# Moving the experts' ranks and marks, and the layer norm's small steps, from VectorE to GpSimd

## The reference

```python
x = x + 0.5 * _L0_ffn_ref(_layernorm(x), ...)      # F
x = x + _L0_attn_ref(_layernorm(x), ...)           # R
x = x + 0.5 * _L0_ffn_ref(_layernorm(x), ...)      # F
x = x + 0.5 * _L1_ffn_ref(_layernorm(x), ...)      # E
x = x + _L1_attn_ref(_layernorm(x), ...)           # M
x = x + 0.5 * _L1_ffn_ref(_layernorm(x), ...)      # E
```

```python
logits = jnp.einsum('bsd,ed->bse', x, router_w) + router_b
probs = jax.nn.softmax(logits, axis=-1)
weights = jnp.max(probs, axis=-1)
top1 = jnp.argmax(probs, axis=-1)
y_all = jnp.einsum('bsd,eod->bseo', x, expert_w) + expert_b
y = jnp.take_along_axis(y_all, top1[:, :, None, None], axis=2)[:, :, 0, :]
out = y * weights[:, :, None]
```

## Time and the profile before

| | us |
|---|---|
| median of 3 runs | 1591.86 (1585.59 to 1592.55) |
| profiled execution, own time | 1587.52 |
| its span, first to last instruction | 1585.8 |
| granted TensorE clock, mean | 0.993 |

### The profile page before, as it was taken

How to read it: one execution, slowest core, us unless ns; L and a number is a source line. 1 busy time by engine, 2 the same in 40 slices (tenths; PEclk the granted TensorE clock), 3 DMA queues, 4 the chain that set the end, 5 groups by cost and what they waited for, 6 DMA issues and landing times. The chain is left out here.

```text
span 1585.8 us, 43554 instructions
## 1 busy us (share of the span) xinstructions
PE 1527.1 (96%) x15760; PEld 910.0 (57%) x15760; DVE 1264.2 (80%) x2662; ACT 934.4 (59%) x1826; POOL 934.7 (59%) x806
## 2 busy tenths in 40 slices
PE   7999999999999899799999999999998899999998
PEld 4666666666666666566666666666663334444443
DVE  7976777777877788786776777768779889999968
ACT  6755555555655433365555555556553378888843
POOL 2865756657664299875756657657446334444454
PEclk9999999999999999999999999999999899999999
DMA  4300000000001243200000000000001212111112
GB/s 163 104 11 5 7 0 7 7 0 7 5 5 34 46 83 76 42 5 5 8 1 7 7 0 7 3 4 8 2 15 28 47 36 61 36 42 46 26 35 67
DMA packets 74636, 43.40 MB, mean 27 GB/s; under 512 B 54106, under 2 KB 71162, under 8 KB 74372
## 3 DMA queue, kind: packets, MB, share of 16 engines
q1 hardware_dynamic: 74500, 41.60, 10.9%
HBM read 10.47 MB, written 2.10 MB: 8 GB/s over the span
## 5 line engine op out<-in xcount | busy, mean ns | idle before, releaser
L642 POOL TENSOR_TENSOR scratch<-scratch 128x512 f16<-128x512 f32 x379 | 440.9, 1164 | 375.4 <-ACT scratch L850 375.0
L845 ACT ACTIVATE scratch<-psum 128x512 f32<-128x512 f32 x512 | 305.2, 597 | 398.0 <-PE psum L2008 397.1
L1420 DVE SCALAR_TENSOR_TENSOR scratch<-psum,scratch 128x512 f32<-128x512 f32 x512 | 352.4, 689 | 234.8 <-PE psum L2008 212.4
L2050 PE MATMUL psum<-ffn_down_hi,scratch 128*128 128x128 f16 x2048 | 369.3, 219 | 0.3
L2051 PE MATMUL psum<-ffn_down_lo,scratch 128*128 128x128 f16 x2048 | 369.4, 219 | 0.0
L2052 PE MATMUL psum<-ffn_down_hi,scratch 128*128 128x128 f16 x2048 | 369.4, 219 | 0.0
L850 ACT ACTIVATE scratch<-scratch 128x512 f16<-128x512 f32 x512 | 318.6, 622 | 9.0 <-DVE scratch L1420 8.9
L2050 PEld LDWEIGHTS psum<-ffn_down_hi,scratch 128*128 128x128 f16 x2048 | 200.3, 98 | 58.9 <-DVE scratch L1427 0.5
L2051 PEld LDWEIGHTS psum<-ffn_down_lo,scratch 128*128 128x128 f16 x2048 | 200.4, 98 | 58.1
L2052 PEld LDWEIGHTS psum<-ffn_down_hi,scratch 128*128 128x128 f16 x2048 | 200.4, 98 | 0.0
L2006 PE MATMUL psum<-x_hi,ffn_gate_hi 128*128 (+1 forms) x512 | 194.5, 380 | 1.5 <-ACT scratch L845 1.5
(11 more groups left out here) (230 smaller groups left out, 2663.7 us busy)
## 6 DMA issues: line engine op xcount, KB each, us to landing
scratch<-scratch SPq DMA_DIRECT2D x96, 128.0 KB, 2.7
raw<-in_ffn_w_dram SPq DMA_DIRECT2D x8, 768.0 KB, 4.3
ffn_up_hi<-scratch SPq DMA_DIRECT2D x32, 128.0 KB, 2.8
x_tok<-in_x_dram SPq DMA_DIRECT2D x8, 256.0 KB, 6.8
out_dram<-x_tok SPq DMA_DIRECT2D x7, 256.0 KB, 2.3
raw<-in_lin_dram SPq DMA_DIRECT2D x1, 1092.0 KB
x_hi<-scratch SPq DMA_TRANSPOSE x46, 2.3
x_lo<-scratch SPq DMA_TRANSPOSE x46, 2.3
```

Source lines behind the costliest of these rows:

```text
L642: pool.tensor_tensor(h_lo[r], h32[r], h_hi[r], ALU.subtract).then_inc(s_plo, 1)
L845: act.activation(gate_act[k % 2], bank(k % 2), ACT.Silu, scale=W_DOWN).then_inc(s_s, 1)
L1420: dve.scalar_tensor_tensor(h32[k % HSLOTS], bank(5 + k % 2), W_DOWN, gate_act[k % 2], ALU.mult, ALU.mult).then_inc(s_h, 1)
L2050: pe.matmul(dst, h_hi[r][:, cols], hi, start=k % FC == 0 and n == 0, stop=False, skip_group_check=True)
```

## The change

1. For the batches from 2 on of either E phase, GpSimd makes e_rank (in two instructions: is_ge, then times rev_index) and e_not (`mark_others`, now a subtraction, first minus rank). VectorE keeps the maximum e_first in the same place (`first_of`). For batches 0 and 1 VectorE still does all three. E_OUT falls from 2^14 to 2^12, since the difference replaces a 0 or 1.
2. ln_neg is gone: the norm on GpSimd subtracts the mean as it stands in ln_mv. This holds in R, E and M.
3. In E and M, ln_var is made by GpSimd just ahead of ln_rstd (`prep_rstd(n, True)`).
4. In GpSimd's iteration, `rank`, `x_lower`, `not_chosen` and then `add` follow one another; before it was `add`, `x_lower`.

```diff
-            def prep_rstd(n):
+            def prep_rstd(n, var=False):
+                if var:
+                    pool.wait_ge(s_mv, n + SUB)
+                    pool.tensor_scalar(ln_var[:], ln_mv[:, 1:2 * SUB:2], LN_EPS, None, ALU.add).then_inc(s_var, SUB)
                 pool.wait_ge(s_var, n + SUB)
...
+                def rank(b):
+                    pool.wait_ge(s_esh, b + 1)
+                    pool.wait_ge(s_efirst, b)
+                    pool.tensor_scalar(e_rank, e_shift, 0.0, None, ALU.is_ge).then_inc(s_etop, 1)
+                    pool.wait_ge(s_etop, b // NB * (NB - 2) + b % NB - 1)
+                    pool.tensor_tensor(e_rank, e_rank, con_("rev_index"), ALU.mult).then_inc(s_erank, 1)
+
+                def not_chosen(b):
+                    pool.wait_ge(s_efirst, b + 1)
+                    pool.wait_ge(s_eoutp, b)
+                    mark_others(pool).then_inc(s_enot, 1)
...
                 for b in range(NB):
+                    if b and b + 1 < NB:
+                        rank(use * NB + b + 1)
+                    if b and b + 2 < last:
+                        x_lower(n0 + SUB * (b + 2))
+                    if b and b + 1 < NB:
+                        not_chosen(use * NB + b + 1)
                     if b:
                         add(b - 1)
-                        if b + 2 < last:
-                            x_lower(n0 + SUB * (b + 2))
                     if b + 3 < last:
-                        prep_rstd(n0 + SUB * (b + 3))
+                        prep_rstd(n0 + SUB * (b + 3), True)
                         norm(b + 3)
...
-                if negate:
-                    dve.tensor_scalar(ln_neg[:], ln_mv[:, 0:2 * SUB:2], -1.0, None, ALU.mult)
-                dve.tensor_scalar(ln_var[:], ln_mv[:, 1:2 * SUB:2], LN_EPS, None, ALU.add).then_inc(s_var, SUB)
+                if var:
+                    dve.wait_ge(s_mv, n + SUB)
+                    dve.tensor_scalar(ln_var[:], ln_mv[:, 1:2 * SUB:2], LN_EPS, None, ALU.add).then_inc(s_var, SUB)
...
+                def first_of(b):
+
+                    dve.wait_ge(s_erank, b + 1)
+                    dve.wait_ge(s_enot, b)
+                    dve.tensor_reduce(e_first, by(e_rank, SUB), AX_X, ALU.max).then_inc(s_efirst, 1)
...
-                        if k == 1 and more:
-                            select(b0 + b + 1)
+                        if k == 1 and more and b == 0:
+                            select(b0 + 1)
+                        if k == 1 and more and b:
+                            first_of(b0 + b + 1)
```

More of the change, by code:

```diff
@@ L332, in build, with mark_others @@
         s_erows_in, s_erows, s_ebias = sem("e_rows_loaded"), sem("e_rows_set"), sem("e_bias_rows_placed")
+        s_etop, s_erank, s_efirst = sem("e_at_top"), sem("e_ranked"), sem("e_first_found")
         s_estep = sem("e_routing_step")
-        E_STEPS = 4
+        E_STEPS = 2
+        def mark_others(engine):
+            rank = e_rank.rearrange("p (q o e) -> p q o e", q=SUB, o=1).to_broadcast([P, SUB, P // E_GROUP, E])
+            first = e_first.rearrange("p (q o c) -> p q o c", q=SUB, o=1).to_broadcast([P, SUB, P // E_GROUP, E])
+            return engine.tensor_tensor(e_not.rearrange("p (q o c) -> p q o c", q=SUB, c=E_GROUP)[:, :, :, 0:E], first, rank, ALU.subtract)
         def expert_banks(t):
@@ L692, in norm @@
                     for q in range(SUB):
-                        ins = pool.tensor_scalar(x_norm[:, q * P:(q + 1) * P], sub(x_tok, SUB * (bx % NB) + q), ln_neg[:, q:q + 1],
-                                                 ln_rstd[:, q:q + 1], ALU.add, ALU.mult)
+                        ins = pool.tensor_scalar(x_norm[:, q * P:(q + 1) * P], sub(x_tok, SUB * (bx % NB) + q), ln_mv[:, 2 * q:2 * q + 1],
+                                                 ln_rstd[:, q:q + 1], ALU.subtract, ALU.mult)
                     ins.then_inc(s_xn, SUB)
@@ L1322, in _, with prep_bn @@
         def _(dve):
-            def prep_bn(n, s):
+            def prep_bn(n, s, after=False):
+                if after:
+                    dve.wait_ge(s_mv, n)
                 for q in range(SUB):
@@ L1628, in route @@
                     dve.tensor_tensor(by(e_shift, SUB), by(bank(7, 0, SUB * E), SUB), over(e_max, SUB, E), ALU.subtract).then_inc(s_esh, 1)
+                def first_of(b):
+                    dve.wait_ge(s_erank, b + 1)
+                    dve.wait_ge(s_enot, b)
+                    dve.tensor_reduce(e_first, by(e_rank, SUB), AX_X, ALU.max).then_inc(s_efirst, 1)
                 def select(b):
                     dve.wait_ge(s_esh, b + 1)
[L1633 to L1636, removed]
+                    dve.scalar_tensor_tensor(e_rank, e_shift, 0.0, con_("rev_index"), ALU.is_ge, ALU.mult).then_inc(s_erank, 1)
+                    first_of(b)
+                    dve.wait_ge(s_efirst, b + 1)
                     dve.wait_ge(s_eoutp, b)
-                    rank = e_rank.rearrange("p (q o e) -> p q o e", q=SUB, o=1).to_broadcast([P, SUB, P // E_GROUP, E])
-                    first = e_first.rearrange("p (q o c) -> p q o c", q=SUB, o=1).to_broadcast([P, SUB, P // E_GROUP, E])
-                    dve.tensor_tensor(e_not.rearrange("p (q o c) -> p q o c", q=SUB, c=E_GROUP)[:, :, :, 0:E], rank, first, ALU.not_equal).then_inc(s_enot, 1)
+                    mark_others(dve).then_inc(s_enot, 1)
                 def invert_sum(b):
@@ L1644, in invert_sum @@
                     dve.tensor_reduce(e_sum, by(e_exp, SUB), AX_X, ALU.add).then_inc(s_estep, 1)
-                    step(b, 4)
+                    step(b, 2)
                     dve.wait_ge(s_eprob, b)
```

24 lines of the change are left out of this document (11 added, 13 removed).

## The result

The changed kernel takes 1605.21 us (median of 6 runs, 1603.88 to 1607.45); the kernel before on the same chip takes 1592.12 (6 runs, 1585.59 to 1592.55). The ratio is 1.009, 95% interval 1.0072 to 1.0107: 0.9% slower, where 0.46% faster was forecast. The profiled execution took 1605.68 with a span of 1603.9, 18.1 longer than the span before; the medians differ by 13.1, since the profiled execution of the kernel before was 4.6 faster than its median.

A forecast was written before the change was run, and what follows sets the result against it. The prediction took VectorE to bound the steady E iteration; savings of 4.31 us in the first E phase and 3.04 in the second, 7.35 together, took 1591.86 to 1584.5 us (-0.46%), range 1578.0 to 1589.5.

The forecast's parts named there:

- What GpSimd adds: Step pricing GpSimd's E iteration after the change: 5.2 plus 0.95 and two waits of 0.10, 6.35 us, under 6.98.
- the forecast loop: Steady E iteration after the change, closed over TensorE and VectorE: 6.98 us, with VectorE waiting about 0.5 before the first pick.
- VectorE is the bound of the steady iteration: Step on the kernel before: VectorE has no idle time in the 7.63 us E iteration, TensorE some 0.8 us of room.
- first E phase to batch 7's first pick: Forecast saving of 4.31 us: 3.13 from five loops of 6.98 and 1.18 in the last iteration.
- second E phase, second pick of iteration 1 to the last first pick: Forecast saving of 3.04 us, with iteration 1 losing 0.14 and loops without statistics taking 6.65.
- the moved add delays nobody: In GpSimd's E iteration, the add behind the marks costs nothing, since its batch's store and reuse are a batch away.
- The prediction's other estimate: GpSimd prices by the skill's 2.6 cycles per element at 1.2 GHz: e_not 0.28 us, the product 0.07.
- the slack ahead of `others`: Time by which GpSimd's marks precede TensorE's `others` in E: 0.20 us, some 0.3 by the skill's cycle rule.
- rival (a): GpSimd's small instructions have a fixed part of some 0.3 us, `others` waits 0.40 per loop: 1588.6 us; chance 0.22.
- the limit of 0.98: In the E iteration, GpSimd's three small pieces together must stay within 0.98 us or `others` waits; forecast 0.80.
- (b): Rival: GpSimd's small pieces cost over 0.54 us each, making it slower; at 0.8 each, 1600 us; chance 0.06.
- (d): Rival: VectorE and GpSimd block each other in E, so the move gives nothing: loop 7.6, 1591 us; chance 0.05.

The follow-up runs named there:

- b: Kernel before with part 2 of the change alone (GpSimd's norm subtracts the mean from ln_mv, ln_neg gone): 1604.86 us, ratio 1.0086.
- c: Kernel before with only the operation of GpSimd's norm changed, add to subtract, operand still ln_neg: 1602.69 us, single run.
- d: Kernel before with only the operand of GpSimd's norm changed, from ln_neg to the mean in ln_mv, still an add: 1587.32 us, single run.
- e: Changed kernel with GpSimd's norm adding the mean from ln_mv instead of subtracting it: 1582.79 us, ratio 0.9964.
- j: Changed kernel with multiply and add in GpSimd's norm in place of subtract and multiply: 1580.04 us, single run.
- k: Changed kernel with multiply and then subtract in GpSimd's norm in place of subtract and multiply: 1608.4 us, single run.
- l: Kernel before with a quarter of GpSimd's norm left out (three of four pieces): 1580.03 us, single run.
- i: Kernel before with ln_var and ln_neg moved to GpSimd, ranks and marks still on VectorE, norm adding ln_neg: 1592.05 us, ratio 1.0025.
- h: Kernel before with ranks and marks moved to GpSimd, ln_neg and ln_var still on VectorE, norm adding ln_neg: 1584.0 us, ratio 0.9981.
- g: f with the add of iteration 6 of the first E phase put behind the power and the norm: 1583.3 us, ratio 0.9973.
- f: Changed kernel with GpSimd itself making ln_neg and the norm adding it, computing the reference's outputs: 1582.49 us, ratio 0.9962.
- m: g with batch 2 of the second E phase ranked and marked by VectorE instead of GpSimd: 1582.97 us, ratio 0.9973.

## Why the prediction was wrong

**The step that failed.** The part "What GpSimd adds" put GpSimd's iteration together "from starts (1.12 + 1.70 + 1.22 + about 1.12)" plus 0.95. The 1.70 is the norm in its old form. Part 2 of the change gives it another operation; the prediction counted of this part only that ln_neg leaves VectorE. The four pieces start to start take 3.11, 1.41 more. With it GpSimd's work is 7.98 an iteration (8.32 less 0.34), above the forecast loop's 6.98, and with the 0.34 that x_lower waits for ScalarE it becomes the bound; ranks and marks come late because the norm ahead of them ends late. b, c, d, e, j and k show it: the operation alone makes 447 into 792, and without it the same change is 0.36% faster. The price was not to be had from the rows ahead of the prediction (the one subtraction among GpSimd's, x_lower, is no slower than the add), but the operation had changed, and the step should have had two ends: nothing, and something like the 0.544 piece of the earlier trace rows.

**The second step, hidden by the first.** "VectorE is the bound of the steady iteration" was not so. Its row has no idle time, but 0.37 of e_rank was a block, and this block closed a ring through GpSimd: ln_var, power, norm, add, x_lower, the end of e_rank, then e_first, e_not, pick, statistics and ln_var again. From ln_var's end (1209.53) to e_rank's (1206.73 + 7.63 + 0.56 = 1214.92) is 5.39, and from there to the next ln_var's end 2.24 (1209.53 - 1207.29): 7.63. l takes 0.43 from GpSimd's share and gains 0.38 of it. b adds 1.40 to it; the block moves on to e_not, past 0.55 of VectorE's share (e_rank's end, 1207.29, to e_not's, 1207.84), and e_not ends 0.14 after x_lower where e_rank ended 0.04 after it. So the ring is 7.63 + 1.40 + 0.10 - 0.55 = 8.58, and 8.60 was measured. i puts 0.26 more between bn_aggr and the power (1209.30 to 1210.35, for 1208.89 to 1209.68), and 7.63 + 0.26 = 7.89 for the measured 7.92, though VectorE was relieved. The Trainium skill, "SBUF — State Buffer", section "Who interferes with whom", states that a VectorE instruction with two SBUF inputs contends with a GpSimd instruction that reads SBUF, and that `tensor_scalar` can as well, in the modes that use both of VectorE's ports. The traces agree with what it says of two inputs: e_rank, e_not and L1902 have two and were held, the reductions and bn_stats nowhere. ln_neg, a `tensor_scalar`, was held in h; no run shows in which mode it ran.

**What held.** With the norm's form put right (e), the rest of the forecast can be read:

| step | forecast | measured in e |
|---|---|---|
| steady iteration, VectorE's wait in it | 6.98, 0.5 | 6.99, 0.48 |
| first E phase to batch 7's first pick | -4.31 | 51.76 for 56.07, -4.31 |
| from there to its last pick | 0 | 8.80 for 6.43, +2.37 |
| second E phase, second pick of iteration 1 to the last first pick | -3.04 | 40.77 for 43.09, -2.32 |
| to attention's seventh x_tok | 0 | 262.21 for 260.82, +1.4 |

Executions of one kernel also scatter ahead of the first pick: it stands at 1185.25 in e, 1187.02 before and 1190.21 in b, so spans are compared from there.

The third row is the sentence "the moved add delays nobody": it delays the last norm, x_upper and with it the q and k copies by 0.9 (in g 1.0 came back), and 1.5 are the clock: from the products' start to the pick it is 3.33 in e (1242.48 to 1245.81) and 1.83 before (1247.69 to 1249.52). In the second E phase iteration 1 lost 0.54 instead of 0.14, and the first iteration without statistics took 6.95 instead of 6.65. Of the fifth row, 1.2 are no effect of the change: the step from the sixth x_tok to the seventh took 31.7 for 30.5, and so it did in d, where nothing moved. Over its six us from 1502 the granted clock was 1.00 before and in f, 0.72 in d and 0.50 in h. The five iterations ahead of it are 31.29 each for 31.36, 0.35 less. The remaining 0.5 lie ahead of the first x_tok (74.07 from the last pick for 73.54); j has 73.60 there and m 74.10, so no run shows whether they belong to the change. The window of h:

```profile
1502.00:1508.00 6.00, 6.00 (x53) 1.66 (x51) 2.05 (x8) 3.35 (x8) 4.06 (x8) 0.50 0.00 1
```

**The small pieces.** The four were put at 0.95 together. From start to start e shows 0.39 and 0.20 for the halves of e_rank and 0.36 for e_not; with 0.38 for ln_var that is 1.33. The prediction's other estimate, 0.28 for e_not and 0.07 for the product, is further off, and by its own working the slack ahead of `others` would have been 0.4 and not 0.3, since each of the two is 0.10 less. A 128x4 instruction takes 0.23, so there is a fixed part, as rival (a) had it; still the three small pieces make 0.95, under the limit of 0.98, and `others` does not wait in e.

**The rivals.** The time ended nearest to (b), 1600, and at its place, since `others` waits 1.15 for the marks; but not by its mechanism, for the small pieces were under its 0.54. (d) had the right mechanism, the block, and the wrong sign: it was in the kernel before, and moving e_rank and e_not away is what released it. That explains why the parts do not add up: h gains 0.32 an iteration, i loses 0.3, and both together gain 0.64, for h still has ln_neg in the way (0.60 of block on VectorE's 6.70 make its 7.3) and i still has e_rank.

**What stays open.** Why a wait of TensorE costs the clock in one execution and a longer one doesn't in another. Why VectorE's small instruction in attention is held by one mask in b and by two in the changed kernel; the traces show only that it starts at another place. And whether the last 1 us between e, f, g and m is real: their ratios, 0.9962 to 0.9973, overlap.

## What to carry to other kernels

Price an instruction again when only its operation changes, with engine, shape and bytes the same; if no row shows the new form, measure it by itself first. An engine without idle time is not yet the bound: where one of its instructions is longer than its like and ends with another engine's instruction, the ring runs through that one, and relief for the engine that seems to idle is what counts. A change of several parts is worth taking apart even when it is slower: here it held a gain of 0.4% and a loss of 1.3% (1.009 for 0.9964; the same operation on the kernel before costs 0.9%).

## What the runs showed of the hardware

- GpSimd's two-operation instruction with scalars from SBUF, 128x128 f32: add and multiply 447 ns, multiply and add 449, subtract and multiply 792 to 797, multiply and subtract 797 (medians; means for j and k). In R, b's pieces have a median of 797 but reach 1.34 us. VectorE's own norm has the subtract as well and takes 344 ns in the kernel before (median; up to 1.32 us). A subtraction of two inputs of 128x512 takes 1.16 us on GpSimd, an add 1.27.
- GpSimd's small instructions, duration: 128x4 0.23, 128x32 comparison 0.31, 128x32 product 0.24, 128x128 difference of two broadcast inputs 0.40 us; start to start, with the wait of the next on it, up to 0.39.
- A VectorE instruction of 0.17 to 0.30 us took 0.56 to 1.19 beside GpSimd's, ending within 0.14 of the end of a GpSimd instruction, in attention at times of the second one (once it took 2.06, to the end of the fourth).
- TensorE's granted clock was 0.51 behind a wait of 4.37 in the changed kernel and 0.50 behind one of 2.40 in e, and it stayed at 1.00 behind one of 2.94 in f.
